# Four casts moved from ScalarE to VectorE, two scales and a conversion ordered earlier at the end of attention, and the last raw load made to wait, in a fused attention and quantized-MLP kernel

## What is computed

```python
def attention(up, down, Wq, Wk, Wv, Wskip):
    q, k, v = Wq @ up, Wk @ down, Wv @ down
    p = softmax(q.T @ k / sqrt(128))
    return Wskip @ up + (p @ v.T).T

def mlp(x):                     # 4-bit weights, a scale and a zero for 64 inputs
    Wg, Wu, Wd = ((nibbles(W) - zero) * scale for W in (gate, up, down))
    return Wd @ (silu(Wg @ x) * (Wu @ x))     # 1024 -> 2752 -> 1024

x = x + attention(layernorm(x), ctx)
x = x + mlp(layernorm(x))
```

## Time and profile before

| | us |
|---|---|
| Median of 3 runs | 1407.02 (1406.82 to 1407.9) |
| The profiled execution: its time | 1410.28 |
| The profiled execution: its span | 1408.1 |
| PE busy | 1386.9 (98%) |
| DVE busy | 1117.1 (79%) |
| ACT busy | 689.6 (49%) |
| POOL busy | 310.2 (22%) |

### The profile page before, as it was taken

How to read it: one execution, slowest core, us unless ns; L and a number is a source line. 1 busy time by engine, 2 the same in 40 slices (tenths; PEclk the granted TensorE clock), 3 DMA queues, 4 the chain that set the end, 5 groups by cost and what they waited for, 6 DMA issues and landing times.

```text
span 1408.1 us, 19597 instructions
## 1 busy us (share of the span) xinstructions
PE 1386.9 (98%) x6414; PEld 677.3 (48%) x6414; DVE 1117.1 (79%) x1598; ACT 689.6 (49%) x1279; POOL 310.2 (22%) x365
## 2 busy tenths in 40 slices
PE   8999998999999999999999999999999999999999
PEld 6676764444444444444444444444444444444443
DVE  6888978887877877878778788788788788788376
ACT  6899984344344444344444444343444444444330
POOL 1132332122122122122222212212222212212200
PEclk9999999999999999999999999999999999999999
DMA  6222222286486576576576666756846746748596
GB/s 191 101 102 86 83 90 61 53 157 120 97 147 122 103 134 123 105 138 118 105 136 111 126 118 119 136 108 116 146 95 124 129 108 123 126 100 154 98 299 261
DMA packets 58982, 174.83 MB, mean 124 GB/s; under 512 B 8000, under 2 KB 11072, under 8 KB 54592
## 3 DMA queue, kind: packets, MB, share of 16 engines
q0 software_dynamic: 34560, 83.90, 38.4%
q1 hardware_dynamic: 24096, 90.20, 20.9%
q10 hardware_dynamic: 288, 0.26, 0.1%
HBM read 73.67 MB, written 100.66 MB: 124 GB/s over the span
## 4 chain that ended last, share of the span: by engine, by line
PE 91%; DVE 4%; ACT 2%; issue 2%; POOL 0%; DMA 0%; SPq 0%; DVEq 0%; POOLq 0%; ACTq 0%
PE ps L590 52%; PE ps L628 9%; PE ps L629 9%; PE ps L630 9%; PE ps L553 3%; PE ps L523 2%; PE ps L793 2%; PE ps L511 2%; PE ps L752 1%; PE ps L548 1%; PE ps L542 1%; ACT temps L859 1%; ACT temps L833 1%; DVE stats L1263 0%; DVE neg_max L1294 0%
## 5 line engine op out<-in xcount | busy, mean ns | idle before, releaser
L590 PE MATMUL ps<-xt,w_gu 128*128 128x512 f16 x3528 | 796.1, 379 | 5.7 <-DVE temps L1510 1.7
L590 PEld LDWEIGHTS ps<-xt,w_gu 128*128 128x128 f16 x3528 | 344.8, 98 | 422.7 <-ACT temps L939 2.6
L972 ACT ACTIVATE stage<-ps,pow 128x512 f32<-128x512 f32 x300 | 204.3, 687 | 323.6 <-PE ps L630 317.6
L1540 DVE SCALAR_TENSOR_TENSOR stage<-ps,pow,stage 128x512 f32<-128x512 f32 x220 | 160.1, 747 | 106.1 <-ACT stage L972 67.2
L628 PE MATMUL ps<-park 128*128 128x512 f16 x560 | 212.9, 380 | 2.0 <-ACT stage L972 2.0
L629 PE MATMUL ps<-park 128*128 128x512 f16 x560 | 213.0, 380 | 0.0
L630 PE MATMUL ps<-park 128*128 128x512 f16 x560 | 212.9, 380 | 0.0
L437 POOL DMA_DIRECT2D out<-stage x80 | 70.6, 883 | 429.0 <-DVE stage L1540 429.0
L451 POOL DMA_DIRECT2D out<-stage x80 | 69.2, 865 | 296.4 <-ACT stage L972 296.4
L969 ACT CAST park<-temps 128x512 f16<-128x512 f32 x140 | 83.2, 615 | 64.8 <-DVE temps L1524 38.1
L1537 DVE TENSOR_TENSOR park<-temps,park 128x512 bf16<-128x512 f32 x140 | 98.3, 708 | 17.0 <-ACT park L969 14.0
(11 more groups left out here) (137 smaller groups left out, 1623.4 us busy)
## 6 DMA issues: line engine op xcount, KB each, us to landing
out<-stage POOLq DMA_DIRECT2D x80, 512.0 KB, 5.3
out<-stage POOLq DMA_DIRECT2D x140, 256.0 KB, 5.3
grid<-grids SPq DMA_DIRECT2D x136, 256.0 KB, 6.1
raw<-packed SPq DMA_DIRECT2D x34, 512.0 KB, 4.2
out<-stage SPq DMA_DIRECT2D x16, 512.0 KB, 2.6
stage<-x SPq DMA_DIRECT2D x12, 512.0 KB, 3.6
xt<-out SPq DMA_DIRECT2D x12, 512.0 KB, 12.1
out<-xt SPq DMA_DIRECT2D x12, 512.0 KB, 2.6
```

The lines of the kernel that those rows point to most:

```text
L590: mm = pe.matmul(bank, w_gu[e][:, wp, w, P * j:P * j + P], xt[:, xb, xp, j, cols], start=(fresh and n == 0), stop=(n == 3 * J - 1), skip_g ...
L972: return act.activation(dst, ps[:, bank, :], ACT.Copy, scale=pow2[:, 10:11])
L1540: return dve.scalar_tensor_tensor(out=part, in0=ps[:, bank, :], scalar=pow2[:, 10:11], in1=part, op0=ALU.mult, op1=ALU.add)
```

## The change

SP waits for all copies with `s_r7` ahead of the raw words of job 32. The high parts of job 0 are cast by DVE and not by ACT: two casts in step 9, two in step 13. In `first_tile`, job 1's two scales move from behind `LATE[0]`'s block to both sides of the last `normalize`; what followed them moves up by a place; and ACT does `plain_hi(2, 1)` a place earlier, ahead of `silu0`. At the end, DVE does `c22_out` ahead of `last_nibbles(0)`.

```diff
@@ SP @@
             load_grid(3 * PAIRS + 2, 6 * PAIRS + 4)
+            sp.wait_ge(s_r7, 8 * PAIRS)
             load_raw(3 * PAIRS + 2, 12 * PAIRS + 6)
@@ ACT @@
             for i in range(STEPS):
                 step(i)
-                if i == 9:
-                    plain_hi(0, 0)
-                elif i == 13:
-                    mixed_hi(0, 0, 0)
-                    mixed_hi(0, 0, 1)
...
-                if at == 2:
+                if at == 1:
                     plain_hi(2, 1)
@@ DVE @@
+            def first_hi(first, n, src, done, count):
+
+                dve.wait_ge(done, count)
+                dve.tensor_copy(w_half(0, 0, first, n), src).then_inc(s_weight_hi, 1)
+
+            def first_plain_hi():
+                first_hi(W11, 1, q0, s_weight, 1)
+                first_hi(W12, 2, r, s_weight, 2)
+
+            def first_mixed_hi():
+                first_hi(S2, 2, q, s_comb, 3)
+                first_hi(S4, 2, r, s_comb, 4)
+
             first_job = {
+                9: first_plain_hi,
...
-                13: lambda: second_sums(0),
+                13: lambda: (second_sums(0), first_mixed_hi()),
...
                 if at == 1:
                     row_stats(1, B - 1)
+                    times_scale(q, 3, 6)
                     normalize(1, B - 1)
+                    times_scale(r, 4, 6)
                     block_done(LATE[0])
-                if at == 2:
-                    job_scale(1, 6)
                 if at in (3, 4):
                     block_done(LATE[at - 1])
+                if at == 2:
+                    plain_lo(1, 4)
                 if at == 3:
-                    plain_lo(1, 4)
+                    first_sums(4, 4)
                 if at == 4:
-                    first_sums(4, 4)
                     second_sums(4)
...
+            c22_out(n0 + 1)
             last_nibbles(0)
-            c22_out(n0 + 1)
             last_weights(0)
```

## The result

The changed kernel takes 1409.74 us (median of 22 executions, 1409.09 to 1415.1), the kernel before 1407.40 us beside it (22 executions, 1406.7 to 1409.28): a ratio of 1.002, 95% interval 1.0014 to 1.0026. It is 2.3 us slower; the forecast was 1.5 us faster, 1405.5, with a range up to 1408.2. The profiled execution of the change took 1411.51 us (span 1409.7), that of the kernel before 1410.28 (span 1408.1). Further down, one execution of the kernel before (3803 us) and one of a changed kernel (6364 us) are left out of every number.

What follows compares the result with a forecast made beforehand. PE, busy 98% of the span, was taken to bound the kernel; -2.6 + 0.2 + 0 + 0.9 = -1.5 us, put onto the median 1407.02, gave 1405.5 us. Own range 1402.8 to 1408.0; 8 in 10, 1401.5 to 1408.2.

Steps and rivals of the forecast that it cites:

- What bounds the kernel: Whole kernel: PE is busy 98% of the span, so only its waits and clock losses at four places count.
- the gap to the median: Profiled 1410.28 us stands 3.3 over the median 1407.02; put down to profiling, so the same difference applies to the median.
- the old wait: Behind the loop: PE waits 1.98 us for ACT's copy ending at 1328.52, then loses 1.7 us by the clock.
- Part 1: Attention, steps 9 and 13: four casts move to DVE, ending PE's waits for ACT's copies; -2.6 us.
- the whole of it: Attention: all 2.6 us that five steps take too long would be regained by moving the casts to DVE.
- Part 2: First MLP tile, job 1's scales: PE's first wait becomes 2.6 us, later work comes earlier; +0.2, between -0.7 and +1.0.
- Part 3: Job 32's raw load and `c22_out`: no wait of PE shortened, delays covered with 0.9 us to spare; cost 0.
- Part 4: Behind the loop: shifted instruction counts remove PE's 1.98 us wait and add 2.9 us before `p7`; +0.9 us.
- number 833: Place in DVE's and ACT's instruction lists where each waits on instructions behind the loop, 3.19 and 4.39 us.
- the loss of clock behind it I take as equal: Behind the loop: the new wait before `p7` loses the same clock as the removed one, 1.7 us away, 1.7 back.
- its three terms: The forecast's own range: clock in the first tile, PE's new wait, clock behind either wait; given as 1402.8 to 1408.0.
- DVE too full: Rival, chance 0.12, attention: a cast delays a maximum or `normalize` for PE, the casts' gain is lost; 1407 to 1408.

Runs made afterwards that it cites:

- part 2 alone: Only the two `first_tile` hunks (job 1's scales, ACT's earlier `plain_hi(2, 1)`) on the kernel before: 1410.71 us against 1407.47.
- part 3 alone: Only SP's wait ahead of job 32's raw words and `c22_out` ahead of the nibbles, on the kernel before: 1407.74 us against 1407.47.
- four and eight idle writes: Kernel before with four or eight one-column writes added at the start of DVE's list: 1410.88 us (before 1407.38) and 1412.39 us (before 1407.55).
- the three kernels with this wait: The change, 1409.74 us; its `first_tile` hunks alone on the kernel before, 1410.71; the change with DVE's instruction count restored, 1407.62.
- the kernel with the `lo` earlier: Kernel before plus the four DVE casts, DVE's instruction count restored, plain `lo` ahead of `LATE[2]`'s block, first sums ahead of `c22_out`: 1404.32 us against 1407.77.
- part 1 alone: Only the four casts moved from ACT to DVE, on the kernel before: 1408.62 us against 1407.47.
- part 1 and the old count: Kernel before plus the four DVE casts, six reductions merged and one idle write added so DVE's list keeps its length: 1405.44 us against 1407.38.
- the wait of 2.10 us: Kernel before plus the four DVE casts, DVE's instruction count restored, only job 1's first scale ahead of the last `normalize`: 1407.78 us against 1407.38.

## Why the prediction was wrong

**What bounds the kernel; the gap to the median.** "3.3 us over the median 1407.02, which I put down to profiling" is, in the order of the text, the first step that failed. The profiled execution of before was an unusual one: its clock fell behind PE's wait, where 92 of 95 timed executions kept 1.000 throughout. The wait itself, 1.98 us, was the longest of five: part 2 and part 3 alone had 0.80 and 1.15, four and eight idle writes 1.79 and 1.81. Its rest took 1107.72 us against 1104.85 and 1105.20; without any wait it is 1103.87, in five kernels. So the old wait cost 1.0 and 1.3 us in those two executions, and 1.8 by its length in the other two, with the clock kept; not 3.7. That is all that ACT's four fewer instructions can give back.

**Part 1, -2.6.** Right in kind: 12.41 us per step, casts of 0.37 and 0.69 us, the reciprocals at 124.77 and 177.03 (forecast 125.1 and 177.4). The size was -1.8: one step still takes 13.21 us (183.09 to 196.30), with a wait of 0.54 us for the same copy. ACT's timeline shows what holds it up: the copy comes straight behind a normalization that waits for DVE's reciprocal.

```profile
183.22 1.71 ACT L860 ACTIVATE temps<-temps,inv_total 128x256 f32<-128x256 f32 x4 [0.82 <-DVE inv_total L1332]
```

DVE is never idle from 171 to 183 us there, and the reciprocal stands behind a `normalize`. So the term failed where it took "the whole of it": 0.8 us went back to a full DVE. Whether the casts of step 13 alone do that was not tried.

**Part 2, +0.2.** This step failed by most, and alone takes the forecast out of its range: the kernel with part 2 alone is 3.2 us slower than before, and the tile takes 2.6 to 2.8 us more. The start, 222.18 less the 1.87 us of attention, would have been 220.3; PE came at 223.26, 2.9 us late, where I had 1.3. Three pieces make that up. The second scale's own 1.2 us were in the sum. The first scale stands beside POOL's one-column sum, which then takes 1.05 us and not 0.19, so `normalize` starts 0.9 us late and not 0.1. And the second scale stands beside POOL's two sums and takes 2.17 us and not 1.2. The clock then fell always (44 of 44 executions of the three kernels with this wait were below 1.000), and not half of the time: 1.7 us. What the order pays back was right: PE was 4.6 us late with the lost clock and 2.8 late at tile 1, so 1.9 came back, against 2.0 in the sum. Only it can be had without the price, as the kernel with the `lo` earlier shows. The trace of before had the warning, and I took no row for it. POOL's timeline in attention has a one-column operation at two lengths, and DVE's and POOL's at the end of the loop have a scale of only 512 columns at 1.76 us:

```profile
150.81 1.42 POOL L401 TENSOR_TENSOR rstd<-var_eps,neg_half 128x1 f32<-128x1 f32 x1
...
154.68 0.55 POOL L401 TENSOR_TENSOR rstd<-var_eps,neg_half 128x1 f32<-128x1 f32 x1
```

```profile
1294.38 1.76 DVE L1391 SCALAR_TENSOR_TENSOR quant<-quant,pow,grid 128x512 f32<-128x512 f32 x1
```

```profile
1293.83 1.77 POOL L467 TENSOR_TENSOR temps<-temps 128x512 f32<-128x512 f32 x1 [3.23 <-DVE temps L1530]
```

The Trainium skill, SBUF — State Buffer, section "SBUF: two separate sides", says that a DVE operation with two SBUF sources and a GpSimd operation that reads SBUF exclude one another for the whole instruction. The runs agree: the sum on POOL ends with the first scale (217.53 and 217.48), the second scale finishes 1.1 us after POOL's pair (221.92 and 220.84), and a scale with POOL idle takes 1.27.

**Part 3, 0.** Right, by the kernel that has it alone.

**Part 4, +0.9.** Right in place and in nature: "issue" before `fourth_sum`, a wait before `p7`, none at 1329, and four and eight idle writes put it where number 833 stands. PE's wait was 2.01, 2.39, 2.25 and 2.93 us: under the forecast's 2.5 to 3.6 in three of four, the changed kernel's among them. That PE's stretch "rest" is equal in the two profiles, 1107.72 and 1107.75, is luck: in each a wait of 2.0 us stands with a lost clock behind it, which the old wait usually has not. What failed is "the loss of clock behind it I take as equal". The new wait makes the rest 1106.30 to 1106.43 us with the clock kept and 1107.75 with it lost, against 1104.85 to 1105.20 for the old one: about +1.3, and +2.7 where it is lost (in part 1 alone, 5 of 11 executions were below 1.000).
The Trainium skill, Runtime: NRT & Kernel Launch, section on instruction fetch mechanics, calls the crossing of a block "mostly hidden". Here it is not: DVE stood still for 2.75 to 4.09 us in each of the thirteen profiles, hidden only where nobody waited for that instruction.

**The end, not in the sum.** With four more instructions the last packet of instructions runs beside the last store, which lands 0.66 us later: in all four kernels with that count, and in none of the other nine. That the packet delays the store fits all thirteen, but was not tried in another way. With the 0.4 us less outside the span, the end costs the time 0.3 us.

**The sum anew**, for usual executions: -1.8 + 2.7 + 1.3 to 2.7 + 0.3 = 2.5 to 3.9 us slower. Measured: 2.3. Medians of the other kernels stand within about 1.4 us of such sums; the start of the execution, which scatters by 4 us in the profiles, may be the rest of it, but that stays open. Open is also why the clock holds behind a wait of 2.4 us in one execution and falls behind 2.0 in another. The prediction's own range was also added up too narrow: its three terms (-0.9 or +0.8, -0.4 or +0.7, 1.7 either way) give 1402.5 to 1408.7, not 1402.8 to 1408.0, and 1409.74 lies outside both.

The rivals: "DVE too full" came nearest in time (1407 to 1408) but is not what happened; attention kept 1.8 of its 2.6 us. The step to slower was in the forecast's own two terms, parts 2 and 4.

## What to carry to other kernels

Before work is put into an engine's gap, look at what runs in that gap on the engine that it shares memory access with: here a 1.2 us scale made a 0.19 us sum on GpSimd the critical wait, and moving other, later work into an idle stretch took 1.8 us off the tile at no price that a profile shows. Count instructions ahead of a loop: idle instructions that compute nothing cost 3.5 us by where they put the wait on instructions behind it, and one merged instruction won 2 to 3 us. And read a profile's clock and waits against several executions before a wait in it is booked as a gain.

## What was not expected of the hardware

- A wait of PE costs more than its length once the clock falls behind it. In the kernel with part 1 and the old count (a wait of 1.24 us in the tile) 8 of 11 executions kept 1.000, with the wait of 2.10 us 4 of 11, and with 4.2 us none of 44. One fall cost 1.7 us in the tile, and 3.4 us in one execution behind the loop.
- One DVE list position, number 833, carried the wait in every kernel: 2.75 to 4.09 us.
- With a packet of instructions beside it the last store landed 0.66 us later, in four kernels of four.
- A DVE cast with one source slowed as well beside POOL: 1.65 us and not 0.69.
